# Attention and FFN kernel: low parts of W ahead of tile 0's gate, tile 0's LoRA inside tile 1, and tile 1's y transposed by DMA

## The chip, the cores and the metric

The kernel runs on one core of one Trainium2 chip. The metric is the device time of one execution in microseconds, and smaller is better. One core has a matrix engine (PE), a vector engine (DVE), a scalar engine (ACT), GpSimd (POOL) and SyncE (SP), which here issues nearly all transfers.

## The reference

With x of (2, 512, 1024) and ctx of (2, 1024, 1024), the reference quantises, multiplies, and then adds a linear layer with a mixture of eight rank-16 LoRA experts, of which each row uses two:

```python
q1 = fake_quant(layernorm(x)); q2 = fake_quant(ctx)      # uint8 grids, scale and zero point are inputs
x1 = x + q1 @ q2
y = layernorm(x1)
logits = y @ W_router.T; top 2 of 8 experts, their softmax weights renormalised -> combine (row, expert)
h = einsum('nd,erd->ner', y, A_stack) * combine[..., None]
out = x1 + y @ W_base.T + b_base + 2.0 * einsum('ner,eor->no', h, B_stack)
```

## The kernel before

The 1,024 rows are cut into eight tiles of 128 rows (T = 8), and the 1,024 columns of the contraction into eight slices k (K = 8). Every engine has its own instruction stream, written out by hand. An engine executes its stream in order, and semaphores hold an instruction until what it names has happened. So the order of the calls in each engine's block is the schedule.

**Stage 1** makes x1. For each tile PE multiplies the transposed quantised x (`a1_t`) with the quantised ctx (`product`), DVE takes the sum out of PSUM into `xs` (`sum_x1`), and either DVE or POOL adds a correction that depends on the column (`add_corr`).

**Stage 2** multiplies y with W. To get more than 16 bits of precision, y and W are each split into a rounded half (`_hi`) and the rest (`_lo`), both float16, and `wide(t, k)` issues six matmuls of 512 columns: hi·hi, hi·lo and lo·hi, for each half of the output. `narrow(t)` does the same against A and the router (`ar_hi`, `ar_lo`, 136 columns, 24 matmuls). From its result DVE works out the gate (`gate_tile`, 14 small instructions) and the weighted LoRA rows `hc`. PE transposes `hc` (`transpose_hc`), ACT and DVE split it (`split_hct`), and `lora(t)` multiplies it with B (six matmuls of 512 columns), into the same PSUM banks as `wide`.

**W's halves.** Eight slices of W lie in `stage`. When the largest value is known (`peaks_w` on DVE, one PE matmul, `scale_w` on DVE), ACT rounds each slice (`split_w` on ACT writes `w_hi`) and DVE makes the rest (`split_w` on DVE writes `w_lo`). For tile 0, PE takes slice k when `w_lo` of k is there.

**The way of y.** DVE measures a tile's mean and variance (`statistics_y`), POOL turns them into a scale and a bias (`scale_y`), and ACT makes y (`make_y`). For tiles 0 and 1, PE transposes y in float32 and ACT and DVE split the transposed tile (`split_first_yt`, `split_yt`). From tile 2 on, ACT rounds y (`round_y` writes `y_hi`), DVE makes the rest (`rest_y` writes `y_lo`; both lie in the buffer `a1_t`, so the trace names them a_t), and SP sends each half through a transposing DMA into `yt_hi` and `yt_lo`, which raises `y_hi_turned` and `y_lo_turned`.

Each output tile is closed by DVE: `add_bias` adds bias and a row term to `xs`, `sum_out` adds the PSUM banks, and SP stores it.

Of the kernel before, what the change touches and what calls it, by code (L numbers as in the profile page):

```python
# [5 lines left out]
P = 128  # L6
# [23 lines left out]
def xattn_ffn(nc, x, ctx_kv, quant, w_t, bias, ar_t, b_t, out):  # L30
# [20 lines left out]
    with ExitStack() as stack:  # L51
# [86 lines left out]
        HCT = slice(256, 256 + P)  # L138
# [3 lines left out]
        FIRST_ADDS = 3  # L142
# [48 lines left out]
        @block.sync  # L191
        def _(sp):
            def load_x(t):
                sp.dma_start(xs[:, t, :], x_tiles[t]).then_inc(x_in[t], 16)

            def load_staged(n):
                if n >= RING:
                    sp.wait_ge(ctx_ready, n - RING + 1)
                src = ctx_tiles[n] if n < N else w_tiles[n - N]
                sp.dma_start(stage[:, n % RING, :], src).then_inc(stage_in[n % RING], 16)  # L200

            def transpose_y(t):
                sp.wait_ge(out_done, t - 1)
                sp.wait_ge(y_hi_ready, t - 1)
                sp.dma_start_transpose(out=yt_hi[:, t % 2, :, :], in_=y_hi).then_inc(y_hi_turned, 16)
                sp.wait_ge(y_lo_ready, t - 1)
# [36 lines left out]
        def _(pool):
# [68 lines left out]
            scale_y(0, 2)  # L312
            pool.wait_ge(b_lo_ready, 1)
            add_corr(3)
            scale_y(2, 3)
            add_corr(4)
            scale_y(3, 4)
            for t in range(5, T):
                add_corr(t)
                scale_y(t - 1, t)  # L320
# [3 lines left out]
        def _(act):  # L324
# [52 lines left out]
            def make_y(t):  # L377
                act.wait_ge(y_scaled, t + 1)
                if t > 0:
                    act.wait_ge(y_transposed, min(t, 2))  # L380
                if t > 2:
                    act.wait_ge(y_lo_ready, t - 2)
                nc.scalar.activation(y[:, :], xs[:, t, :], ACT.Identity, bias=y_bias[:, t:t + 1],  # L383
                                     scale=y_scale[:, t:t + 1]).then_inc(y_ready, 1)
# [7 lines left out]
            def split_yt(t):  # L392
                act.wait_ge(y_transposed, t + 1)
                nc.scalar.activation(yt_hi[:, t % 2, :, :].rearrange("p (h k) c -> p h (k c)", h=2),
                                     ps[:, YT_BANKS, :], ACT.Copy).then_inc(yt_hi_ready, 1)

            def round_y(t):
                if t > 2:
                    act.wait_ge(y_hi_turned, 16 * (t - 2))
# [8 lines left out]
            def split_hct(t):  # L408
                act.wait_ge(hc_transposed, t + 1)
                nc.scalar.activation(hct_hi[:, :], ps[:, AR_BANK, HCT], ACT.Copy).then_inc(hct_hi_ready, 1)  # L410
# [24 lines left out]
            make_y(1)  # L435
            split_b()
            for k in range(3, K):
                split_w(k)
            gate_weight(0)
            split_yt(1)  # L440
# [3 lines left out]
            for t in range(1, T):  # L444
                gate_weight(t)
                if t + 1 < T:
                    make_y(t + 1)
                    round_y(t + 1)
                split_hct(t)
# [4 lines left out]
        def _(dve):  # L454
# [168 lines left out]
            def split_yt(t):  # L623
                def halves(a):
                    return a.rearrange("p (h k) c -> p h (k c)", h=2)

                dve.wait_ge(yt_hi_ready, t + 1)
                nc.vector.tensor_tensor(halves(yt_lo[:, t % 2, :, :]), ps[:, YT_BANKS, :],
                                        halves(yt_hi[:, t % 2, :, :]), ALU.subtract).then_inc(yt_lo_ready, 1)

            def rest_y(t):
                dve.wait_ge(stage1_done, T)
                dve.wait_ge(y_ready, t + 1)
                dve.wait_ge(y_hi_ready, t - 1)
                if t > 2:
                    dve.wait_ge(y_lo_turned, 16 * (t - 2))
# [136 lines left out]
        def _(pe):  # L773
# [160 lines left out]
            pe.wait_ge(y_hi_turned, 16 * (last - 1))  # L934
            pe.wait_ge(y_lo_turned, 16 * (last - 1))
# [37 lines left out]
```

## Time and profile before

| what | value |
|---|---|
| median of 3 runs | 171.85 us (171.85 to 171.87) |
| the profiled execution | 171.81 us |
| its span, from first to last instruction | 170.0 us |
| around the span | 1.81 us |
| busy: PE, DVE, ACT, POOL | 158.2, 118.9, 74.1, 59.9 us |

The profiled execution stands 0.04 us below the median. Times in rows are microseconds from the span's start. In a timeline, a row is a run of instructions of one line: start, duration from the first start to the last end, engine, line, operation, output and input, count, and in brackets the idle time of the engine before it and what ended it. Matmuls overlap: a matmul of 512 columns shows 0.38 us, but the next one starts earlier than its end.

### The profile page before, as it was taken

Reading aid. Unit: us, or ns where it says so; the run is one execution under the profiler, and the core shown is the slowest. Engines: PE = TensorE matmul, PEld = TensorE weight load, DVE = VectorE, ACT = ScalarE, POOL = GpSimd, SP = SyncE. Lnnn points to the kernel's source line nnn. Section 1 sums busy time; section 2 is a strip of 40 time slices with the busy share of each in tenths; the row PEclk is TensorE's granted clock in tenths of the full one; section 3 lists DMA queues with packets and bytes.
Section 4 is the critical chain, followed back from the end, with each engine's and each line's share of the span. In section 5 each row is a group of like instructions: output and inputs, shape, how many; then the busy total and the mean of one; then the engine's idle time right before and its main releaser. Section 6 shows DMA issues by size and latency. Waiting matters only on the chain.

```text
span 170.0 us, 2585 instructions
## 1 busy us (share of the span) xinstructions
PE 158.2 (93%) x922; PEld 83.6 (49%) x922; DVE 118.9 (70%) x276; ACT 74.1 (44%) x100; POOL 59.9 (35%) x140
## 2 busy tenths in 40 slices
PE   6977898899989799799999999999999999999992
PEld 3543344345535356364554564564555556456541
DVE  7993939999998999996919908908907826804802
ACT  3096509799996994506217007105305305300000
POOL 8905476887840000187082081082050050000000
PEclk9999999999999999999999999999999999999998
DMA  4999999999930000000352250350360360360311
GB/s 111 387 416 413 406 409 407 406 411 413 407 151 2 0 0 4 0 0 0 75 177 41 46 160 10 72 169 0 62 185 4 62 185 0 62 185 6 123 62 62
DMA packets 19452, 25.89 MB, mean 152 GB/s; under 512 B 13552, under 2 KB 13808, under 8 KB 19440
## 3 DMA queue, kind: packets, MB, share of 16 engines
q1 hardware_dynamic: 19296, 25.73, 43.4%
q8 instruction: 7, 0.11, 0.3%
q14 instruction: 5, 0.04, 0.1%
q10 hardware_dynamic: 144, 0.00, 0.0%
HBM read 18.38 MB, written 4.19 MB: 133 GB/s over the span
## 4 chain that ended last, share of the span: by engine, by line
PE 62%; DVE 19%; issue 6%; POOL 5%; ACT 4%; DMA 2%; DVEq 0%; ACTq 0%; POOLq 0%
PE ps L835 37%; PE ps L795 10%; PE ps L825 5%; DVE w_lo L606 2%; PE ps L786 2%; DVE xs L541 2%; ACT w_hi L370 2%; DMA yt_lo<-a_t 2%; PE ps L816 2%; PE ps L817 2%; PE ps L818 2%; POOL root L262 2%; PE ps L780 1%; DVE bnx L472 1%; DVE bnx L470 1%
## 5 line engine op out<-in xcount | busy, mean ns | idle before, releaser
L835 PE MATMUL ps<-w_hi,yt_hi 128*128 128x512 f16 x128 | 39.5, 380 | 1.7 <-DVE w_lo L606 1.2
L835 PE MATMUL ps<-w_lo,yt_hi 128*128 128x512 f16 x128 | 39.4, 379 | 0.0
L835 PE MATMUL ps<-w_hi,yt_lo 128*128 128x512 f16 x128 | 39.4, 379 | 0.0
L795 PE MATMUL ps<-a,a_t 128*128 128x512 f16 x128 | 31.2, 379 | 2.3 <-DVE a_t L534 1.5
L406 ACT ACTIVATE gate<-gate,ar_undo 128x1 f32<-128x1 f32 x8 | 2.4, 295 | 55.9 <-DVE gate L643 55.9
L331 ACT ACTIVATE a<-stage,prm,inv_s 128x1024 uint8<-128x1024 f32 x16 | 19.4, 1241 | 9.4 <-DMA stage<-in_ctx_kv 9.3
L642 DVE MAX8 top<-ps 128x8 f32<-128x8 f32 x8 | 1.4, 173 | 27.5 <-PE ps L818 27.5
L835 PEld LDWEIGHTS ps<-w_hi,yt_lo 128*128 128x128 f16 x128 | 12.5, 98 | 15.1
L795 PEld LDWEIGHTS ps<-a,a_t 128*128 128x128 f16 x128 | 11.9, 98 | 16.2 <-DVE a_t L534 3.0
L835 PEld LDWEIGHTS ps<-w_lo,yt_hi 128*128 128x128 f16 x128 | 12.5, 98 | 14.7
L250 POOL TENSOR_TENSOR xs<-xs,corr 128x1024 f32<-128x1024 f32 x5 | 11.8, 2363 | 22.2 <-DVE b_lo L612 22.2
L835 PEld LDWEIGHTS ps<-w_hi,yt_hi 128*128 128x128 f16 x128 | 11.6, 98 | 14.9 <-issue 2.8
L261 POOL TENSOR_SCALAR root<-mvy 128x1 f32<-128x1 f32 (+1 forms) x7 | 1.5, 218 | 38.8 <-DVE mvy L466 38.7
L816 PE MATMUL ps<-ar_hi,yt_hi 128*128 128x136 f16 x64 | 11.7, 223 | 0.2 <-DMA yt_lo<-a_t 0.2
L817 PE MATMUL ps<-ar_lo,yt_hi 128*128 128x136 f16 x64 | 11.7, 223 | 0.0
L818 PE MATMUL ps<-ar_hi,yt_lo 128*128 128x136 f16 x64 | 11.7, 223 | 0.0
L383 ACT ACTIVATE y<-xs,y_bias,y_scale 128x1024 f32<-128x1024 f32 x8 | 9.8, 1228 | 1.8 <-POOL y_bias L289 1.8
L671 DVE SCALAR_TENSOR_TENSOR xs<-xs,row_term,bias_sb 128x1024 f32<-128x1024 f32 x8 | 10.3, 1285 | 0.3
L786 PE MATMUL ps<-a,ones 128*128 128x512 f16 x32 | 9.5, 379 | 0.9 <-ACT a L331 0.9
L606 DVE SCALAR_TENSOR_TENSOR w_lo<-stage,scale,w_hi 128x1024 f16<-128x1024 f32 x8 | 10.0, 1279 | 0.2 <-ACT w_hi L370 0.2
L541 DVE SCALAR_TENSOR_TENSOR xs<-ps,con,xs 128x1024 f32<-128x1024 f32 x8 | 10.1, 1268 | 0.0
L262 POOL TENSOR_TENSOR root<-root,minus_half 128x1 f32<-128x1 f32 (+1 forms) x13 | 9.7, 744 | 1.1
(135 smaller groups left out, 262.4 us busy)
## 6 DMA issues: line engine op xcount, KB each, us to landing
stage<-in_ctx_kv SPq DMA_DIRECT2D x16, 512.0 KB, 13.2
stage<-in_w_t SPq DMA_DIRECT2D x8, 512.0 KB, 10.7
xs<-in_x SPq DMA_DIRECT2D x7, 512.0 KB, 13.2
out_dram<-xs SPq DMA_DIRECT2D x7, 512.0 KB, 3.0
ar_raw<-in_ar_t SPq DMA_DIRECT2D x1, 544.0 KB, 16.3
xs<-in_x SPq DMA_DIRECT2D x2, 256.0 KB, 3.8
b_raw<-in_b_t SPq DMA_DIRECT2D x1, 512.0 KB, 11.3
bias_sb<-in_bias SPq DMA_DIRECT2D x1, 512.0 KB, 12.1
```

Source lines behind the costliest of these rows:

```text
L250: nc.gpsimd.tensor_tensor(xs[:, t, :], xs[:, t, :], corr[:, t // TB, :], ALU.add).then_inc(x1_ready, 1)
L262: then(nc.gpsimd.tensor_tensor(guess, whole, minus_half[:, w], ALU.pow))
L331: nc.scalar.activation(low_bytes(a2[:, n, :]), stage[:, n % RING, :], ACT.Identity, bias=prm[:, 3:4], scale=inv_s[:, 2:3]).then_inc(ctx_re ...
L541: nc.vector.scalar_tensor_tensor(out=xs[:, t, :].rearrange("p (h n) -> p h n", h=NH), in0=ps[:, s1_bank(t):s1_bank(t) + 2, :], scalar=s12, ...
L606: nc.vector.scalar_tensor_tensor(out=w_lo[:, k, :], in0=stage[:, k, :], scalar=scale[:, 2:3], in1=w_hi[:, k, :], op0=ALU.mult, op1=ALU.sub ...
L671: nc.vector.scalar_tensor_tensor(out=xs[:, t, :], in0=xs[:, t, :], scalar=row_term[:, t:t + 1], in1=bias_sb[:, :], op0=ALU.add, op1=ALU.ad ...
L786: last = nc.tensor.matmul(ps[:, COLSUM_BANK + h, :], ones16[:, 0:P], a2[:, b * K + k, h * H:(h + 1) * H], start=k == 0, stop=k == K - 1)
L795: last = nc.tensor.matmul(ps[:, s1_bank(t) + h, :], a1_t[:, t % 4, k, :], a2[:, n, h * H:(h + 1) * H], start=k == 0, stop=k == K - 1)
L816: nc.tensor.matmul(dst, yt_hi[:, p, k, :], ar_hi[:, k, :], start=k == 0, stop=False)
L817: nc.tensor.matmul(dst, yt_hi[:, p, k, :], ar_lo[:, k, :], start=False, stop=False)
L818: last = nc.tensor.matmul(dst, yt_lo[:, p, k, :], ar_hi[:, k, :], start=False, stop=k == K - 1)
L835: ins = nc.tensor.matmul(ps[:, OUT_BANK[p] + h, :], part, rhs[:, k, h * H:(h + 1) * H], start=k == 0 and part is hi and rhs is w_hi, stop= ...
```

## The change

Seven things change together:

- Tile 1's y no longer goes through PE. It takes the way of the later tiles: `round_y(1)` on ACT, `rest_y(1)` on DVE, two transposing DMAs on SP. `split_yt` is gone from ACT and DVE.
- `add_corr(2)` moves from DVE to POOL, and on POOL `scale_y(t - 1)` now stands ahead of `add_corr(t)` for t = 3 and 4 as well.
- On DVE, `take_a1t(7)` moves ahead of `peaks_w`; `split_ar` moves from ahead of the first `split_w` to behind the fourth; and all eight `split_w` now stand ahead of `gate_tile(0)`, with `rest_y(1)` among them.
- On ACT, `split_b` moves behind the last `split_w`, and for t = 1 alone `split_hct(1)` moves ahead of `make_y(2)`.
- On PE, `narrow(0)` moves from behind slice 3 to behind slice 5, `transpose_hc(0)` and `lora(0)` move into tile 1, and `narrow(1)` moves from ahead of tile 1 to behind its slice 2. `transpose_hc(1)` moves from behind slice 2 to behind slice 6, and `lora(1)` to the end of tile 1.
- For t = 1, DVE does `split_hct(1)` ahead of `sum_out(0)`.
- The transposed `hc` gets a bank of its own, and six filling matmuls ahead of stage 2 become two.

```diff
-        HCT = slice(256, 256 + P)
+        HCT_BANK = 3
+        HCT = slice(0, P)
...
-        FIRST_ADDS = 3
+        FIRST_ADDS = 2
...
             def transpose_y(t):
-                sp.wait_ge(out_done, t - 1)
-                sp.wait_ge(y_hi_ready, t - 1)
+                if t >= 2:
+                    sp.wait_ge(out_done, t - 1)
+                sp.wait_ge(y_hi_ready, t)
...
             sp.dma_start(bias_sb[:, :], bias.partition_broadcast(P)).then_inc(bias_in, 16)
+            transpose_y(1)
...
             scale_y(0, 2)
+            pool.wait_ge(w_diag_ready, 1)
+            add_corr(2)
             pool.wait_ge(b_lo_ready, 1)
-            add_corr(3)
-            scale_y(2, 3)
-            add_corr(4)
-            scale_y(3, 4)
-            for t in range(5, T):
+            for t in range(3, T):
+                scale_y(t - 1, t)
                 add_corr(t)
-                scale_y(t - 1, t)
...
             make_y(1)
+            for k in range(3, 6):
+                split_w(k)
+            round_y(1)
+            for k in range(6, K):
+                split_w(k)
             split_b()
-            for k in range(3, K):
-                split_w(k)
             gate_weight(0)
-            split_yt(1)
             split_hct(0)
             sum_row(0)
             sum_row(1)
             for t in range(1, T):
                 gate_weight(t)
+                if t == 1:
+                    split_hct(t)
                 if t + 1 < T:
                     make_y(t + 1)
                     round_y(t + 1)
-                split_hct(t)
+                if t > 1:
+                    split_hct(t)
...
             scale_ar()
-            add_corr(2)
             sum_x1(5)
+            take_a1t(7)
             peaks_w()
-            take_a1t(7)
             scale_w()
-            split_ar()
             sum_x1(6)
             split_w(0)
             split_first_yt()
             split_w(1)
             split_w(2)
             split_w(3)
+            split_ar()
+            split_w(4)
             sum_x1(7)
...
-            split_w(4)
             split_w(5)
+            rest_y(1)
+            split_w(6)
+            split_w(7)
             dve.wait_ge(expert_ready, 1)
             gate_tile(0)
-            split_w(6)
-            split_w(7)
             split_hct(0)
             split_b()
-            split_yt(1)
             statistics_y(2)
             add_bias(0)
             for t in range(1, T):
                 gate_tile(t)
-                sum_out(t - 1)
-                split_hct(t)
+                if t == 1:
+                    split_hct(t)
+                    sum_out(t - 1)
+                else:
+                    sum_out(t - 1)
+                    split_hct(t)
...
-            keep_busy(6, 5)
+            keep_busy(2, 5)
...
                 wide(0, k, False)
-                if k == 3:
+                if k == 5:
                     pe.wait_ge(x1_summed, T)
-                    pe.wait_ge(yt_lo_ready, 1)
                     pe.wait_ge(ar_lo_ready, 2)
                     narrow(0)
+
+            pe.wait_ge(y_hi_turned, 16)
+            pe.wait_ge(y_lo_turned, 16)
+            for k in range(K):
+                wide(1, k, False)
+                if k == 1:
+                    transpose_hc(0)
+                if k == 2:
+                    narrow(1)
                 if k == 3:
-                    transpose_y(1)
-                if k == 5:
-                    transpose_hc(0)
-            pe.wait_ge(b_lo_ready, 1)
-            lora(0, stop=True)
-
-            for t in range(1, T - 1):
-                if t == 1:
-                    pe.wait_ge(yt_lo_ready, 2)
...
+                    pe.wait_ge(b_lo_ready, 1)
+                    lora(0, stop=True)
+                if k == 6:
+                    transpose_hc(1)
+            lora(1, stop=True)
```

ACT's stream of before, from tile 0's gate weight on. Here `gate` is the gate weight, `hct_hi` is `split_hct`, `junk,rowsum` is `sum_row`, `y` is `make_y` and `a_t` is `round_y`; the last three rows are `make_y(2)`, `round_y(2)` and `split_hct(1)`.

```order
L406 ACTIVATE gate<-gate,ar_undo 128x1 [waits gate_diff]
L394 ACTIVATE yt_hi<-ps 128x1024 [waits y_transposed]
L410 ACTIVATE hct_hi<-ps 128x128 [waits hc_transposed]
L345 ACTIVATE junk,rowsum<-a 128x1024 [waits peaks_act,x_quantised] x2
L406 ACTIVATE gate<-gate,ar_undo 128x1 [waits gate_diff]
L383 ACTIVATE y<-xs,y_bias,y_scale 128x1024 [waits y_transposed,y_scaled]
L402 ACTIVATE a_t<-y 128x1024 [waits y_ready,stage1_done]
L410 ACTIVATE hct_hi<-ps 128x128 [waits hc_transposed]
```

The same place after the change.

```order
L402 ACTIVATE gate<-gate,ar_undo 128x1 [waits gate_diff]
L406 ACTIVATE hct_hi<-ps 128x128 [waits hc_transposed]
L346 ACTIVATE junk,rowsum<-a 128x1024 [waits peaks_act,x_quantised] x2
L402 ACTIVATE gate<-gate,ar_undo 128x1 [waits gate_diff]
L406 ACTIVATE hct_hi<-ps 128x128 [waits hc_transposed]
L384 ACTIVATE y<-xs,y_bias,y_scale 128x1024 [waits y_lo_ready,y_transposed,y_scaled]
L398 ACTIVATE a_t<-y 128x1024 [waits y_ready,stage1_done,y_hi_turned]
```

`split_hct(1)`, which waits for PE to transpose tile 1's `hc`, has moved ahead of `make_y(2)` and `round_y(2)`; the transposed tile's split is gone.

PE's stream of before, from `transpose_hc(0)` to the first matmuls of `narrow(1)`.

```order
L810 MATMUL ps<-ident,hc 128x128
L835 MATMUL ps<-w_hi,yt_hi 128x512 x2
L835 MATMUL ps<-w_lo,yt_hi 128x512 x2
L835 MATMUL ps<-w_hi,yt_lo 128x512 x2
L835 MATMUL ps<-w_hi,yt_hi 128x512 x2
L835 MATMUL ps<-w_lo,yt_hi 128x512 x2
L835 MATMUL ps<-w_hi,yt_lo 128x512 x2
L825 MATMUL ps<-b_hi,hct_hi 128x512 x2
L825 MATMUL ps<-b_lo,hct_hi 128x512 x2
L825 MATMUL ps<-b_hi,hct_lo 128x512 x2
L816 MATMUL ps<-ar_hi,yt_hi 128x136
```

PE's stream after the change, from `transpose_hc(1)` to the first matmul of `narrow(2)`.

```order
L806 MATMUL ps<-ident,hc 128x128
L831 MATMUL ps<-w_hi,yt_hi 128x512 x2
L831 MATMUL ps<-w_lo,yt_hi 128x512 x2
L831 MATMUL ps<-w_hi,yt_lo 128x512 x2
L821 MATMUL ps<-b_hi,hct_hi 128x512 x2
L821 MATMUL ps<-b_lo,hct_hi 128x512 x2
L821 MATMUL ps<-b_hi,hct_lo 128x512 x2
L812 MATMUL ps<-ar_hi,yt_hi 128x136
```

Before, five slices of `wide(1)` and `lora(1)` stood between `transpose_hc(1)` and tile 2; now it is one slice and `lora(1)`.

## Rows read from the trace of the kernel before

**Rows 1.** The page, busy time of each engine (share of the span, instructions)

```profile
PE 158.2 (93%) x922; PEld 83.6 (49%) x922; DVE 118.9 (70%) x276; ACT 74.1 (44%) x100; POOL 59.9 (35%) x140
```

**Rows 2.** Chain that ended last, 78 to 102: start, time, engine and line

```profile
78.02 1.25 ACT y L383
...
80.81 0.28 DVE row_term L667
...
82.31 1.23 DVE a_t L637
83.56 3.03 DMA yt_lo<-a_t
...
86.72 0.22 PE ps L816
...
92.37 3.88 PE ps L835 x18
96.26 1.39 PE ps L825 x6
97.65 2.60 PE ps L835 x12
...
101.67 0.43 PE ps L835 x2
```

**Rows 3.** Timeline around the end of stage 1, three engines

```profile
47.70 1.23 DVE L550 TENSOR_TENSOR xs<-xs,corr 128x1024 f32<-128x1024 f32 x1
...
48.44 0.61 PE L780 MATMUL ps<-ident,a 128*128 128x128 f16 x8
...
51.20 0.23 PE L878 MATMUL ps<-diag,ones_b 128*128 128x128 bf16 x1 [0.85 <-DVE a_t L534]
...
52.79 1.15 ACT L370 ACTIVATE w_hi<-stage,scale 128x1024 f16<-128x1024 f32 x1 [1.25 <-DVE scale L601]
```

**Rows 4.** Timeline of ACT, 57 to 65

```profile
57.11 1.23 ACT L383 ACTIVATE y<-xs,y_bias,y_scale 128x1024 f32<-128x1024 f32 x1
...
59.19 5.30 ACT L370 ACTIVATE w_hi<-stage,scale 128x1024 f16<-128x1024 f32 x5
```

**Rows 5.** Timeline of DVE, 57 to 76

```profile
57.71 2.48 DVE L606 SCALAR_TENSOR_TENSOR w_lo<-stage,scale,w_hi 128x1024 f16<-128x1024 f32 x2
...
65.22 0.17 DVE L642 MAX8 top<-ps 128x8 f32<-128x8 f32 x1
...
67.70 2.47 DVE L606 SCALAR_TENSOR_TENSOR w_lo<-stage,scale,w_hi 128x1024 f16<-128x1024 f32 x2
...
70.29 1.22 DVE L612 TENSOR_TENSOR b_lo<-b_raw,b_hi 128x1024 fp32r<-128x1024 f32 x1
...
75.45 0.17 DVE L642 MAX8 top<-ps 128x8 f32<-128x8 f32 x1
```

**Rows 6.** Timeline, tile 0's `hc` from PE to ACT

```profile
67.90 0.27 PE L810 MATMUL ps<-ident,hc 128*128 128x128 f32 x1
68.21 0.28 ACT L410 ACTIVATE hct_hi<-ps 128x128 fp32r<-128x128 f32 x1 [1.33 <-PE ps L810]
```

**Rows 7.** Timeline of POOL and DVE, `add_corr(5)` beside tile 2's gate

```profile
87.86 2.36 POOL L250 TENSOR_TENSOR xs<-xs,corr 128x1024 f32<-128x1024 f32 x1
...
88.55 0.21 DVE L643 TENSOR_SCALAR gate<-top 128x1 f32<-128x1 f32 x1
...
88.95 1.30 DVE L646 CAST top_f<-top_i 128x8 f32<-128x8 uint32 x1
```

**Rows 8.** Busy time by stretch at the end; the number behind POOL's is the granted clock

```profile
166.50:167.00 0.50, 0.21 (x1) 0.00 (x0) 0.26 (x1) 0.00 (x0) 0.00 (x0) 1.00 0.00 0
...
168.50:169.00 0.50, 0.00 (x0) 0.00 (x0) 0.00 (x0) 0.00 (x0) 0.00 (x0) 0.68 0.80 270
```

**Rows 9.** Line 842, the matmuls of the start, 1 to 4 and 4 to 8: ns min/median/max

```profile
L842 PE MATMUL ps<-ones x9: 503/527/527, 1.4 to 4.0; 128*128 128x384 f16 x9
...
L842 PE MATMUL ps<-ones x24: 326/326/527, 3.7 to 8.0; 128*128 128x384 f16 x24
```

More of the change, by code:

```diff
@@ L202, in transpose_y @@
             def transpose_y(t):
-                sp.wait_ge(out_done, t - 1)
-                sp.wait_ge(y_hi_ready, t - 1)
+                if t >= 2:
+                    sp.wait_ge(out_done, t - 1)
+                sp.wait_ge(y_hi_ready, t)
                 sp.dma_start_transpose(out=yt_hi[:, t % 2, :, :], in_=y_hi).then_inc(y_hi_turned, 16)
-                sp.wait_ge(y_lo_ready, t - 1)
+                sp.wait_ge(y_lo_ready, t)
                 sp.dma_start_transpose(out=yt_lo[:, t % 2, :, :], in_=y_lo).then_inc(y_lo_turned, 16)
@@ L379, in make_y @@
                 if t > 0:
-                    act.wait_ge(y_transposed, min(t, 2))
-                if t > 2:
-                    act.wait_ge(y_lo_ready, t - 2)
+                    act.wait_ge(y_transposed, 1)
+                if t > 1:
+                    act.wait_ge(y_lo_ready, t - 1)
                 nc.scalar.activation(y[:, :], xs[:, t, :], ACT.Identity, bias=y_bias[:, t:t + 1],
@@ L390, in split_first_yt @@
                                          ps[:, YT_BANKS.start + h, :], ACT.Copy).then_inc(ready, 1)
[L392 to L395, printed above, removed]
             def round_y(t):
-                if t > 2:
-                    act.wait_ge(y_hi_turned, 16 * (t - 2))
+                if t > 1:
+                    act.wait_ge(y_hi_turned, 16 * (t - 1))
                 act.wait_ge(stage1_done, T)
@@ L409, in split_hct @@
                 act.wait_ge(hc_transposed, t + 1)
-                nc.scalar.activation(hct_hi[:, :], ps[:, AR_BANK, HCT], ACT.Copy).then_inc(hct_hi_ready, 1)
+                nc.scalar.activation(hct_hi[:, :], ps[:, HCT_BANK, HCT], ACT.Copy).then_inc(hct_hi_ready, 1)
             act.dma_start(prm[:, :], quant.partition_broadcast(P)).then_inc(quant_in, 16)
@@ L448, in _ @@
                     round_y(t + 1)
-                split_hct(t)
+                if t > 1:
+                    split_hct(t)
                 if t + 1 < T:
@@ L621, in split_first_yt @@
                                             ALU.subtract).then_inc(lo_ready, 1)
[L623 to L629, printed above, removed]
             def rest_y(t):
@@ L633, in rest_y @@
                 dve.wait_ge(y_ready, t + 1)
-                dve.wait_ge(y_hi_ready, t - 1)
-                if t > 2:
-                    dve.wait_ge(y_lo_turned, 16 * (t - 2))
+                dve.wait_ge(y_hi_ready, t)
+                if t > 1:
+                    dve.wait_ge(y_lo_turned, 16 * (t - 1))
                 nc.vector.tensor_tensor(y_lo, y[:, :], y_hi, ALU.subtract).then_inc(y_lo_ready, 1)
@@ L661, in split_hct @@
                 dve.wait_ge(hct_hi_ready, t + 1)
-                nc.vector.tensor_tensor(hct_lo[:, :], ps[:, AR_BANK, HCT], hct_hi[:, :].bitcast(F32),
+                nc.vector.tensor_tensor(hct_lo[:, :], ps[:, HCT_BANK, HCT], hct_hi[:, :].bitcast(F32),
                                         ALU.subtract).then_inc(hct_lo_ready, 1)
@@ L809, in transpose_hc @@
                 pe.wait_ge(hc_ready, t + 1)
-                nc.tensor.transpose(ps[:, AR_BANK, HCT], hc[:, :], ident[:, :]).then_inc(hc_transposed, 1)
+                nc.tensor.transpose(ps[:, HCT_BANK, HCT], hc[:, :], ident[:, :]).then_inc(hc_transposed, 1)
             def narrow(t):
@@ L904, in _ @@
                 wide(0, k, False)
-                if k == 3:
+                if k == 5:
                     pe.wait_ge(x1_summed, T)
-                    pe.wait_ge(yt_lo_ready, 1)
                     pe.wait_ge(ar_lo_ready, 2)
                     narrow(0)
-                if k == 3:
-                    transpose_y(1)
-                if k == 5:
-                    transpose_hc(0)
-            pe.wait_ge(b_lo_ready, 1)
-            lora(0, stop=True)
-            for t in range(1, T - 1):
-                if t == 1:
-                    pe.wait_ge(yt_lo_ready, 2)
-                else:
-                    pe.wait_ge(y_hi_turned, 16 * (t - 1))
-                    pe.wait_ge(y_lo_turned, 16 * (t - 1))
+            pe.wait_ge(y_hi_turned, 16)
[6 more added lines that the diff above has]
+                    narrow(1)
+                if k == 3:
+                    pe.wait_ge(b_lo_ready, 1)
[3 more added lines that the diff above has]
+            lora(1, stop=True)
+            for t in range(2, T - 1):
+                pe.wait_ge(y_hi_turned, 16 * t)
+                pe.wait_ge(y_lo_turned, 16 * t)
                 narrow(t)
-                if t >= 2:
-                    pe.wait_ge(out_summed, t - 1)
+                pe.wait_ge(out_summed, t - 1)
                 for k in range(K):
@@ L933, in _ @@
             last = T - 1
-            pe.wait_ge(y_hi_turned, 16 * (last - 1))
-            pe.wait_ge(y_lo_turned, 16 * (last - 1))
+            pe.wait_ge(y_hi_turned, 16 * last)
+            pe.wait_ge(y_lo_turned, 16 * last)
             narrow(last)
```

## The prediction

> **What bounds the kernel now.** I read the busy time of the engines first: PE works 158.2 of 170.0 us [rows 1], so time can only come from the 12 us in which it stands. Then the chain that ended last, to see where PE does not lead [rows 2]. From 86.72 on every link is PE's: `narrow(2)` starts there, 18 matmuls of `wide` take 3.88 (one slice of six 1.29), `lora` takes 1.39, the last two slices end at 100.25, and the first `wide` of the next tile starts at 101.67, which makes a `narrow` 1.42. A tile is 8 x 1.29 + 1.42 + 1.39 and a transpose, 13.3 us, and nothing in the diff changes PE's work from tile 2 on. Ahead of 86.72 the link is another: y of tile 2 is made on ACT at 78.02, its rest on DVE at 82.31, the transposing DMA takes 3.03, and then PE starts. So the question is where the start of `narrow(2)` moves.
>
> **The end of stage 1.** PE stands 0.85 ahead of the matmul of line 878 at 51.20, for the a1_t that DVE takes late [rows 3]. DVE does `add_corr(2)` from 47.70 for 1.23 first. With that gone and `take_a1t(7)` ahead of `peaks_w`, it can take the tile when PE's transposes end, 48.44 + 0.61 = 49.05. PE's own earlier products last until about 50.3, so 0.9 is gained and no more. From line 878 to ACT's first `w_hi` lie 1.59 (51.20 to 52.79), so that starts at 51.9. POOL's `add_corr(2)`, 2.36 like the one of [rows 7], runs from 50.3 to 52.7; POOL stands idle there in any case.
>
> **DVE's queue.** `sum_x1(6)` starts at 51.8 and the first `w_lo` at 53.05, when `w_hi` is there (51.9 + 1.15). An instruction of 1,024 columns starts 1.20 behind the last (two in 2.48 [rows 5]), and so do the two halves of tile 0's y. That brings DVE to its fourth `w_lo` at 57.85. ACT has by then made `w_hi` 0, tile 0's halves, `w_hi` 1 and 2, and y(1) (1.23 [rows 4], 1.1 until the next start), and makes slice 3 from 57.3 to 58.45 (1.15, five in 5.30 [rows 4]): DVE waits 0.6. Then come slice 3, `split_ar` (two instructions over 1,088 columns, 1.4 at the same rate and with a second start), slice 4, `sum_x1(7)` and slice 5, whose result is there at 64.85; `rest_y(1)` ends at 66.0; slices 6 and 7 end at 68.3, and only there does `gate_tile(0)` start. Before it was 65.22 [rows 5]. That is -0.9, +1.1 for `rest_y(1)`, +2.4 for two `w_lo`, +0.5 for the longer wait.
>
> **PE in tiles 0 and 1.** It is fed by `w_lo` and stands in pieces of up to 1.3 us until slice 5 starts at 64.9. Slice 5, `narrow(0)` and two slices are 3 x 1.29 + 1.42: PE is at 70.2. y(1)'s rest has landed at 66.0 + 3.03 + 0.14 = 69.2, so the new wait is hidden by 1.0; if that cover were gone, each microsecond would count. Removing the eight transposes of y(1) and four filling matmuls costs and gives nothing by itself, as PE waits for `w_lo` anyway. In tile 1 follow two slices (72.8), `transpose_hc(0)`, a slice, `narrow(1)` (75.6), a slice (76.9), `lora(0)` (78.3) and three slices: `transpose_hc(1)` starts at 82.2. Two more waits could delay it. DVE does `split_hct(0)` at 73.4, 0.6 behind the transpose (0.31 to ACT, 0.28 there [rows 6]), and `b_lo` (1.22) is ready at 74.9, wanted at 76.9. From `b_lo`'s start to the next gate were 5.16 (70.29 to 75.45 [rows 5]), now less by `split_yt`; so `gate_tile(1)` starts by 78.8 and, with 2.5 for a gate (65.22 to 67.70), `hc` is there by 81.4. Both fit.
>
> **The new wait.** The order rows of ACT show `split_hct(1)` ahead of `make_y(2)`. An engine executes in order, so y(2), whose scale is ready near 80.2 (from `b_lo`'s start at 73.6 the same way as 70.29 to 78.02, less 1.1 for `split_yt`), is not begun before PE has transposed `hc(1)` at 82.2; before, `make_y(2)` went at 78.02 with four slices of PE's work behind it still to come. Queued behind the waiting `split_hct` are `make_y(2)` and `round_y(2)`; on DVE, behind its own `split_hct(1)`, are `sum_out(0)`, `add_bias(1)` and `rest_y(2)`. From PE's transpose on: 0.31 to ACT, 0.28 `hct_hi`, 0.21 `hct_lo` on DVE, 1.20 `sum_out(0)`, 1.50 from the row term to the rest of y (80.81 to 82.31), 1.23 `rest_y(2)`, and 3.18 from its end (83.54) to PE's start (86.72) [rows 2, 6]. Sum 7.9. ACT's branch (0.31, then y and its rounding, about 2.4) is ready sooner than DVE's 3.5. Meanwhile PE has one transpose, one slice and `lora(1)`, 2.8 us. It then **stands 5.1 us**, and this gap doesn't depend on how early PE comes there. `narrow(2)` starts at 82.2 + 7.9 = 90.1 in place of 86.72: **+3.4**.
>
> After that each tile needs what it needed. In the loop from tile 2 on the order on ACT and DVE is as before; POOL's `scale_y(3)` follows `statistics_y(3)` at the same distance from `narrow(2)`, and the `add_corr` behind it merely moves by a tile. I price these at nothing; the cover is PE's 13.3 us per tile.
>
> **The clock.** At the end of the trace the last matmul ends at 166.71 and the granted clock is full until about 168.68 (a mean of 0.68 over half a microsecond, between 1.00 and 0.50): it fell from 2.4 to 1.2 GHz, 2.0 us after PE's last work [rows 8]. A stand of 5.1 is longer than that. At the start the first matmuls of line 842 last 527 ns up to 4 us and 326 later [rows 9]: about 3.1 us of work, from 1.45 on, went at the lower level, 1.2 GHz. If `narrow(2)` begins in that way, half of 3.1 is lost, **+1.5**. The bounds are 0, if the clock stays up, and 2.5, if the low stretch is as long as the stand itself. I take 1.5, as it is a measured stretch of work behind idleness.
>
> **Sum:** 171.81 (the profiled execution, 0.04 below the median) + 3.4 + 1.5 = 176.7 us.
>
> **The rivals.**
>
> *The clock stays up* through the stand: 171.81 + 3.4 = 175.2. For it: where the clock falls may vary, and two microseconds at the end is one sample. Against it: 5.1 is two and a half times that.
>
> *POOL's `add_corr(2)` holds `scale_w`.* It now runs beside DVE's small instructions that make W's scale. In [rows 7] a cast of 8 elements takes 1.30 and ends with POOL's `add_corr` at 90.2. If the one-element instructions of `scale_w` are held in this way from 50.9 to 52.7, everything behind W's scale is 1.8 later, 171.81 + 3.4 + 1.5 + 1.8 = 178.5. Against it: line 643, with one element, took 0.21 in the middle of the same `add_corr`. The Trainium skill has the rule (SBUF — State Buffer, "Who interferes with whom"): a tensor_scalar in a two-port mode and a GpSimd instruction lock each other out, "the other fully blocks"; by the rule alone the scale would wait and the sum would be this rival's. The trace agrees for the cast and not for one element, so it gets a small chance.
>
> *The clock falls in tile 0 too.* Between 61.1 and 64.9 PE has by my times one slice in 3.8 us, thinner than anything in the trace of before. With a second low stretch: 178.3.
>
> *y(2) is not late,* and the kernel is faster. If `make_y(2)` could start by 77.5, PE would go from the end of tile 1 at 85.0 straight into `narrow(2)`, 1.7 ahead of before: 170.1. For it: in all else PE is ahead. Against it: the order rows; break-even would need `transpose_hc(1)` at 78.8, and even a PE that is never held in tile 0 from 55.0 on, where tile 0's first half is ready, only comes to 78.8.
>
> **How the numbers follow.** The main case has 0.66, the clock that stays up 0.16, POOL's hold 0.06, a second fall of the clock 0.06, the faster case 0.04, and 0.02 is left for no change. A measurement of this kernel tells 0.2% (0.35 us) from nothing. Slower is then 0.94, same 0.02, faster 0.04. The range 174.9 to 178.3 holds the first two cases with 0.3 us for errors in the early times, up to 2.5 for the clock, and the fourth case's middle.
>
> **What the changed kernel's profile would show.** Line 878's counterpart at 50.3; `gate_tile(0)` at 68.3; the DMA of y(1) landed a microsecond before `wide(1)` starts at 70.2; `transpose_hc(1)` at 82.2 with ACT's `make_y(2)` right behind it; PE idle for 5.1 us ahead of `narrow(2)`, released by the DMA of y_lo; a granted clock below 1.00 around 88 to 93; and from the next tile on a period of 13.3. The prediction is wrong if `make_y(2)` starts well before `transpose_hc(1)`, if PE reaches that transpose before 79, or if the clock's loss is not between 0 and 2.5.

## The result, and the profile after

| what | before | after |
|---|---|---|
| median | 171.85 us (171.84 to 171.87) | 177.70 us (176.94 to 177.96) |
| ratio, 95% interval | | 1.0333 (1.0299 to 1.0368) |
| the profiled execution, its span | 171.81, 170.0 us | 176.94, 175.2 us |

The changed kernel is 5.85 us slower; 176.7 was predicted, with a range of 174.9 to 178.3. The profiled execution is the shortest of the four, which matters for the clock below.

The page first, to be held against [rows 1]: the busy time by engine, and TensorE's granted clock in 40 slices of the span.

```profile
PE 157.9 (90%) x910; PEld 83.6 (48%) x910; DVE 116.7 (67%) x275; ACT 74.1 (42%) x100; POOL 61.4 (35%) x141
...
PEclk9999999999999999999978999999999999999999
```

PE does as much work as before in a longer span, so the time is standing time. The two low digits of the clock, slices 21 and 22 of 4.4 us, say where to look. The chain that ended last, 60 to 105, answers to [rows 2].

```profile
64.92 1.15 DVE a_t L630
66.08 4.56 DMA yt_lo<-a_t
...
70.78 2.75 PE ps L831 x12
...
82.94 0.12 PE ps L806
83.09 0.29 ACT hct_hi L406
...
83.61 1.27 DVE xs L670
84.88 0.19 DVE row_term L660
85.09 0.63 DVE xs L664
...
86.30 1.23 DVE a_t L630
87.54 3.04 DMA yt_lo<-a_t
...
90.72 0.27 PE ps L812
```

Read it from the bottom. `narrow(2)` starts at 90.72 and not at 86.72; ahead of it is the DMA of y_lo, ahead of that `rest_y(2)`, `add_bias(1)` (row term and L664), `sum_out(0)` (L670), and ahead of those PE's transpose of `hc(1)` (its matmul starts at 82.78 in the timeline; the chain counts its last part). In [rows 2] no link of PE's stands between 78.02 and the DMA. Now it also has an earlier one: the DMA of tile 1's y_lo, 4.56 us long, ahead of `wide(1)`.

The timeline at the places that the prediction named, with the engine's idle time and what ended it in brackets; these answer to [rows 3, 5, 7].

```profile
50.38 0.22 PE L874 MATMUL ps<-diag,ones_b 128*128 128x128 bf16 x1
...
50.32 2.36 POOL L253 TENSOR_TENSOR xs<-xs,corr 128x1024 f32<-128x1024 f32 x1 [1.81 <-DVE diag L555]
...
51.97 1.15 ACT L371 ACTIVATE w_hi<-stage,scale 128x1024 f16<-128x1024 f32 x1 [0.52 <-DVE scale L602]
...
58.59 1.28 DVE L607 SCALAR_TENSOR_TENSOR w_lo<-stage,scale,w_hi 128x1024 f16<-128x1024 f32 x1 [0.57 <-ACT w_hi L371]
...
68.37 0.16 DVE L635 MAX8 top<-ps 128x8 f32<-128x8 f32 x1
...
83.26 1.23 ACT L384 ACTIVATE y<-xs,y_bias,y_scale 128x1024 f32<-128x1024 f32 x1
...
90.72 0.27 PE L812 MATMUL ps<-ar_hi,yt_hi 128*128 128x136 f16 x1 [4.99 <-DMA yt_lo<-a_t]
...
93.38 0.59 PE L831 MATMUL ps<-w_hi,yt_hi 128*128 128x512 f16 x2
```

The last two rows are the stand and what follows it: `narrow(2)` takes 2.66 us to the first `wide` matmul, where it took 1.42 before. The windows around it show why; the number behind POOL's is the granted clock.

```profile
88.00:90.00 2.00, 0.00 (x0) 0.00 (x0) 0.92 (x3) 0.00 (x0) 0.80 (x3) 0.99 0.82 168
90.00:91.00 1.00, 0.28 (x3) 0.32 (x4) 0.00 (x0) 0.00 (x0) 0.75 (x4) 0.50 1.02 403
91.00:93.00 2.00, 2.00 (x20) 2.00 (x19) 0.00 (x0) 0.00 (x0) 1.74 (x5) 0.50 0.11 45
93.00:94.00 1.00, 1.00 (x9) 0.68 (x7) 0.38 (x4) 0.00 (x0) 1.00 (x1) 0.82 0.06 16
```

While PE stood, the clock fell from 2.4 to 1.2 GHz (at about 89.95: 0.99 is a mean over two microseconds, 1.00 and then 0.50), and it was back at about 93.36. So the 5.13 us that the profiled execution is longer than the one before are a late start of 4.0 and some 1.1 to 1.2 of slow matmuls. The median is 0.7 longer still.

### The profile page after: what moved, and what is told of

Its sections match the earlier page's. It is cut to its first block, busy times and chain, and to the rows that moved or that the text cites. A ratio compares the mean times of both kernels' runs of the same rounds, so it can differ in the third digit from the quotient of the medians.

```text
span 175.2 us, 2567 instructions
## 1 busy us (share of the span) xinstructions
PE 157.9 (90%) x910; PEld 83.6 (48%) x910; DVE 116.7 (67%) x275; ACT 74.1 (42%) x100; POOL 61.4 (35%) x141
## 4 chain that ended last, share of the span: by engine, by line
PE 67%; DVE 16%; DMA 4%; POOL 3%; issue 3%; ACT 3%; DVEq 0%; ACTq 0%; POOLq 0%
PE ps L831 41%; PE ps L791 10%; PE ps L821 6%; DMA yt_lo<-a_t 4%; PE ps L812 2%; PE ps L782 2%; PE ps L813 2%; DVE xs L542 2%; PE ps L814 2%; ACT w_hi L371 2%; DVE w_lo L607 2%; PE ps L776 1%; DVE bnx L473 1%; DVE bnx L471 1%; DVE a_t L630 1%
## 5 line engine op out<-in xcount | busy, mean ns | idle before, releaser
L812 PE MATMUL ps<-ar_hi,yt_hi 128*128 128x136 f16 x64 | 12.8, 234 | 5.0 <-DMA yt_lo<-a_t 5.0
L253 POOL TENSOR_TENSOR xs<-xs,corr 128x1024 f32<-128x1024 f32 x6 | 14.1, 2353 | 1.8 <-DVE diag L555 1.8
L813 PE MATMUL ps<-ar_lo,yt_hi 128*128 128x136 f16 x64 | 12.8, 235 | 0.0
L814 PE MATMUL ps<-ar_hi,yt_lo 128*128 128x136 f16 x64 | 12.8, 234 | 0.0
L664 DVE SCALAR_TENSOR_TENSOR xs<-xs,row_term,bias_sb 128x1024 f32<-128x1024 f32 x8 | 10.3, 1284 | 0.3
```

Source lines behind the costliest of these rows:

```text
L253: nc.gpsimd.tensor_tensor(xs[:, t, :], xs[:, t, :], corr[:, t // TB, :], ALU.add).then_inc(x1_ready, 1)
L664: nc.vector.scalar_tensor_tensor(out=xs[:, t, :], in0=xs[:, t, :], scalar=row_term[:, t:t + 1], in1=bias_sb[:, :], op0=ALU.add, op1=ALU.ad ...
L812: nc.tensor.matmul(dst, yt_hi[:, p, k, :], ar_hi[:, k, :], start=k == 0, stop=False)
L813: nc.tensor.matmul(dst, yt_hi[:, p, k, :], ar_lo[:, k, :], start=False, stop=False)
L814: last = nc.tensor.matmul(dst, yt_lo[:, p, k, :], ar_hi[:, k, :], start=False, stop=k == K - 1)
```

## The experiments

A yardstick for all of them: PE's start of `narrow(2)`, 86.72 before. If nothing behind it changes, the time is 171.81 plus the shift of that start. "Left" is what the profiled execution took beyond that.

| kernel | `narrow(2)` at | by the shift | profiled | left | median (range) |
|---|---|---|---|---|---|
| the changed kernel | 90.72 | 175.81 | 176.94 | 1.13 | 177.70 (176.94 to 177.96) |
| e1, ACT's order of before | 90.29 | 175.38 | 178.11 | 2.73 | 177.75 (177.29 to 178.36) |
| e2, `rest_y(2)` early on DVE | 90.49 | 175.58 | 176.45 | 0.87 | 176.42 (176.32 to 176.90) |
| e3, both edits | 87.56 | 172.65 | 173.55 | 0.90 | 173.57 (173.45 to 173.75) |
| e4, e3 and statistics earlier | 86.20 | 171.29 | 172.47 | 1.18 | 172.47 (172.42 to 172.69) |
| e5, filled stand | 91.13 | 176.22 | 176.12 | -0.10 | 176.12 (175.25 to 176.40) |
| e6, only the end of stage 1 | 86.16 | 171.25 | 171.25 | 0.00 | 171.25 (171.24 to 171.27) |
| e7, scale rows behind the gates | 85.84 | 170.93 | 170.88 | -0.05 | 170.78 (170.56 to 171.06) |
| e8, `transpose_hc(1)` earlier | 89.13 | 174.22 | 175.80 | 1.58 | 175.83 (175.68 to 175.86) |
| e9, e7 with the fetch moved | 85.32 | 170.41 | 170.31 | -0.10 | 170.32 (170.31 to 170.34) |

**Which stream holds y(2)?** e1 restores ACT's order of before and leaves DVE's. e2 leaves ACT's and puts `sum_out(0)` and `rest_y(2)` ahead of DVE's waiting `split_hct(1)`; e3 has both edits. On DVE this is a new order and not that of before, in which `rest_y(2)` stood behind `split_hct(1)` and `add_bias(1)` too.

```diff
 # e1 and e3, ACT
                 gate_weight(t)
-                if t == 1:
-                    split_hct(t)
                 if t + 1 < T:
                     make_y(t + 1)
                     round_y(t + 1)
-                if t > 1:
-                    split_hct(t)
+                split_hct(t)
 # e2 and e3, DVE
-                if t == 1:
-                    split_hct(t)
-                    sum_out(t - 1)
-                else:
-                    sum_out(t - 1)
-                    split_hct(t)
+                sum_out(t - 1)
+                if t == 1:
+                    rest_y(t + 1)
+                split_hct(t)
                 add_bias(t)
-                if t + 1 < T:
+                if 1 < t and t + 1 < T:
                     rest_y(t + 1)
```

> The changed kernel with ACT's order of before for tile 1: make_y(2) and round_y(2) ahead of split_hct(1); DVE's stream is untouched. My theory: the stand of PE ahead of narrow(2) is held by two streams. ACT's part is undone here, but on DVE rest_y(2) still stands behind split_hct(1), sum_out(0) and add_bias(1), so narrow(2) starts 7.9 us behind transpose_hc(1) as in the changed kernel (about 90.7), and the time stays at 177.7 (176.9 to 178.0). Rival: ACT's order alone is the cause, as the prediction's heading of the new wait has it; then y_lo of tile 2 starts at about 83.3, narrow(2) at about 87.7, and the time is near 172.8.

Measured: 177.75 us, ratio 1.0341 (1.0310 to 1.0372). The chain of e1:

```profile
80.36 1.25 ACT y L384
81.71 0.98 ACT a_t L398
82.69 0.25 ACT hct_hi L406
...
83.17 1.28 DVE xs L667
...
84.80 1.07 issue
85.87 1.23 DVE a_t L627
87.11 3.04 DMA yt_lo<-a_t
```

y(2) is made at 80.36, 2.9 earlier than in the changed kernel, and it buys nothing: DVE's `split_hct(1)` still waits for PE, and `sum_out(0)`, the row term, `add_bias(1)` and `rest_y(2)` follow it. `narrow(2)` starts 7.95 behind the transpose, as in the changed kernel (7.94). ACT's new order is not what holds it; DVE's queue is. Of that queue only `sum_out(0)` (L667, 1.28) got behind the wait by the change. With the true order of before on both engines, which no run has, I estimate from this chain a start 7.95 - 1.28 = 6.7 behind the transpose. So by this estimate most of the stand comes from PE's later `transpose_hc(1)`, and the new orders add to it.

> The changed kernel with sum_out(0) and rest_y(2) ahead of split_hct(1) and add_bias(1) on DVE; ACT's stream is untouched. My theory: make_y(2) still starts 0.5 us behind transpose_hc(1), its rounding ends 2.9 behind it, rest_y(2) follows at once, and narrow(2) starts 2.9 + 1.2 + 3.2 = 7.3 behind transpose_hc(1), 0.6 less than in the changed kernel: near 90.1 and a time near 177.1. Rival: DVE's order alone is the cause; then narrow(2) starts near 87.5 and the time is near 172.8.

Measured: 176.42 us, ratio 1.0274 (1.0257 to 1.0291), 0.7 below the expected 177.1. With DVE free, ACT holds; the timeline of e2:

```profile
83.42 1.23 ACT L384 ACTIVATE y<-xs,y_bias,y_scale 128x1024 f32<-128x1024 f32 x1
...
86.02 1.23 DVE L630 TENSOR_TENSOR a_t<-y,a_t 128x1024 f16<-128x1024 f32 x1 [3.86 <-ACT a_t L398]
```

`make_y(2)` starts right behind `hct_hi`, and `narrow(2)` at 90.49. The distance from the transpose (82.94) shrinks only from 7.94 to 7.55, and the start moves by 0.2. The median is 1.3 below the changed kernel's, but most of that I put down to the clock: three of e2's four executions have a mean granted clock of 0.987 to 0.990, and three of the changed kernel's four have 0.981. Of the 0.87 left, 0.37 is a wait of PE for `hc(2)`, of the kind that e3 shows next.

> Both edits: on ACT make_y(2) and round_y(2), on DVE sum_out(0) and rest_y(2), stand ahead of split_hct(1). My theory: make_y(2) then starts when POOL's scale is there, at 80.8, y_hi is there at 83.2, rest_y(2) ends at 84.4 and narrow(2) starts at 87.6. PE stands about 2.2 us in place of 5.3, the clock stays up or loses under 0.5 us, and the time is 172.7 (172.4 to 173.3). Rival: the stand comes from something else (the DMA, POOL); then no more than 0.6 us comes back.

Measured: 173.57 us, ratio 1.0103 (1.0086 to 1.0120). Only with both edits does the start move far, by 3.2, to 87.56. The clock stays at 1.00 and 4.1 of the 5.85 us are gone. That is 0.9 more than the expected 172.7 and outside its range, and the trace of e3 has the place:

```profile
90.39 2.36 POOL L253 TENSOR_TENSOR xs<-xs,corr 128x1024 f32<-128x1024 f32 x1
...
90.85 1.93 DVE L640 TENSOR_SCALAR c<-expert,top_f,gate 128x8 f32<-128x8 f32 x1
92.69 0.20 DVE L641 TENSOR_SCALAR gate<-gate 128x1 f32<-128x1 f32 x1
...
93.80 0.33 PE L801 MATMUL ps<-ident,hc 128*128 128x128 f32 x1 [0.77 <-DVE hc L645]
```

An instruction of 8 elements in tile 2's gate, 0.29 elsewhere, lasts until POOL's `add_corr` is over, and PE waits 0.77 for `hc(2)`. The change did reorder POOL (`scale_y(t - 1)` now stands ahead of `add_corr(t)` for every t from 3 on, not for 3 and 4 alone), but an `add_corr` right behind `scale_y(3)` was there before as well: it began 1.14 behind the start of `narrow(2)` and held a cast of tile 2's gate for 1.30 [rows 7], and PE did not wait. In the changed kernel it is 1.14 again. In e3 it is 2.83 (90.39 against 87.56), since e3 puts `split_hct(1)` and `add_bias(1)` between `rest_y(2)` and `statistics_y(3)`, on which `scale_y(3)` waits. So the new moment comes with e3's own order; how much POOL's reordering has in it is not shown.

**Does an earlier y(2) pay?** e4 is e3 with `statistics_y(2)` and `split_b` ahead of `split_hct(0)`.

> As the third experiment, and on DVE split_b and statistics_y(2) stand ahead of split_hct(0), where the changed kernel lets DVE idle for 3.1 us. My theory: the statistics are there near 73.5, POOL's scale near 77.4, make_y(2) starts there, y_lo is turned before tile 1 ends at 85.5, and narrow(2) starts without a stand of more than 0.2: 85.5 to 85.7 in place of 86.7 in the kernel before, time 170.7 (170.4 to 171.0), faster than before. Rival: a wait that was in the shadow of the stand comes out (gate of tile 1, the sum of tile 0), and the time stays at 171.5 or more.

Measured: 172.47 us, ratio 1.0043 (1.0029 to 1.0057); 170.7 was missed. `narrow(2)` starts at 86.20 (85.5 to 85.7 was expected), 0.5 ahead of the kernel before. But L640 takes 2.09 in tile 1's gate and 2.20 in tile 2's, both begun inside an `add_corr`, and PE waits 1.04 for `hc(2)`. That wait turns the lead over the kernel before into a loss of 0.6.

**Does `add_corr` do that?** e7 is e3 with `statistics_y(2)` ahead of `split_b` and `split_hct(0)`, and with each `add_corr` held until the gate is through:

```diff
-            pool.wait_ge(b_lo_ready, 1)
             for t in range(3, T):
-                scale_y(t - 1, t)
+                pool.wait_ge(hc_ready, t - 2)
                 add_corr(t)
+                scale_y(t - 1, t)
```

> As the fourth experiment, with statistics_y(2) ahead of split_b, and with POOL's add_corr(t) held until hc of tile t - 2 is made and put ahead of scale_y(t - 1). The fourth experiment lost 1.0 us at transpose_hc(2) and 2.1 us in gate 1, each inside add_corr. My theory: with add_corr right behind a gate no small instruction of a gate falls into it, transpose_hc(2) is not waited for, narrow(2) starts at 85.0 to 85.6, and the time is 170.6 (170.2 to 171.0). Rival: the loss at the gates has another cause; then it stays and the time is 172 or more.

Measured: 170.78 us, ratio 0.9939 (0.9922 to 0.9955), and on a second chip 170.83, 0.9945 (0.9928 to 0.9961). This beats the kernel before, though `narrow(2)` starts at 85.84 and not by 85.6. The timeline of e7 at tile 2's gate:

```profile
89.12 0.29 DVE L640 TENSOR_SCALAR c<-expert,top_f,gate 128x8 f32<-128x8 f32 x1
...
90.47 2.37 POOL L253 TENSOR_TENSOR xs<-xs,corr 128x1024 f32<-128x1024 f32 x1 [0.87 <-DVE hc L645]
```

L640 is back at 0.29, PE doesn't wait for `hc(2)`, and nothing is left beyond the shift. The overlap has not gone, it has moved: `b_lo` now takes 2.16 and `rest_y(2)` 1.85 where they took 1.22 or so, each beside an `add_corr`, and there PE has no wait from it.

**What the clock costs.** e5 puts 32 filling matmuls between `lora(1)` and `narrow(2)` of the changed kernel.

```diff
+            keep_busy(32, 6)
             for t in range(2, T - 1):
                 pe.wait_ge(y_hi_turned, 16 * t)
```

> The changed kernel with 32 filling matmuls (384 columns, into a bank that nobody reads any more) between lora(1) and narrow(2): PE works through the stand but nothing arrives sooner. My theory: the stand costs its length (narrow(2) at 90.1 to 90.8 in place of 86.72, +3.4 to +4.0) and the fall of the clock costs the rest of the +5.85. With the fillers the granted clock stays at 1.00, narrow(2) starts where it did, and the time is 175.6 (175.2 to 176.0), with little scatter. Rival: the clock is not what makes the rest (the later tiles are slower for another reason, such as GpSimd's new places); then the time stays at 177 or more.

Measured: 176.12 us, ratio 1.0239 (1.0208 to 1.0270), 0.1 above the expected range. The granted clock stays at 1.00 and the late start alone explains the time, since nothing is left. `narrow(2)` starts at 91.13 and not at 90.72. It is 8.65 behind the transpose (82.48) and not 7.95, because tile 2's two transposing DMAs take 4.7 and 3.7 us here, with a packet of DMA queue q8 between 87.9 and 88.2 (e9 is about that). By the same sum without the clock the changed kernel would take 171.81 + 4.0 = 175.8, so its median holds 1.9 us of clock. This is a remainder: it takes for granted that the other executions start `narrow(2)` at 90.72 too. The plain difference of the two medians is 1.6.

**Is the distance fixed?** e8 is the changed kernel with `transpose_hc(1)` behind slice 5 and not slice 6.

> The changed kernel with transpose_hc(1) one slice earlier, behind slice 5 in place of slice 6. My theory: narrow(2) follows transpose_hc(1) by 7.9 us wherever that stands, so it starts 1.3 us sooner (89.4 beside 90.7), the stand shrinks from 5.3 to about 4.0, and the time falls by 1.3 to 176.4; if the shorter stand also saves the clock, to 174.6. Rival: narrow(2) waits for something that doesn't hang on transpose_hc(1), and the time stays at 177.7.

Measured: 175.83 us, ratio 1.0232 (1.0215 to 1.0249), 0.6 below the expected 176.4. The timeline of e8:

```profile
81.18 0.27 PE L806 MATMUL ps<-ident,hc 128*128 128x128 f32 x1
...
89.13 0.22 PE L812 MATMUL ps<-ar_hi,yt_hi 128*128 128x136 f16 x1 [3.71 <-DMA yt_lo<-a_t]
```

From the transpose to `narrow(2)` it is 7.95 again, so the 1.6 us by which the transpose comes sooner are won in full. The stand shrinks to 3.71 us, and the clock is still at 1.2 GHz from about 89.9 to 93.3. Of the 0.6, 0.3 is `wide(1)`, which starts at 70.48 in place of 70.78.

**What is the end of stage 1 worth alone?** e6 is the kernel before with three edits only: `add_corr(2)` on POOL, `take_a1t(7)` ahead of `peaks_w`, and FIRST_ADDS = 2.

> The kernel before with one part of the change alone: add_corr(2) on POOL as soon as the peak of W is known, and take_a1t(7) ahead of peaks_w on DVE. My theory: the last tile of stage 1 starts on PE 0.8 us sooner (50.4 for 51.20), W's scale with it, everything to the start of narrow(2) moves by that, and the time is 171.0 (170.9 to 171.3). Rival: POOL's add_corr(2) holds the small instructions of scale_w or something behind them; then the time is 171.8 or more.

Measured: 171.25 us, ratio 0.9967 (0.9954 to 0.9979). Of the 0.87 won there (`w_hi` at 51.92 for 52.79), 0.56 reaches `narrow(2)` and the end. The timeline of e6 shows a loss on the way:

```profile
51.86 2.05 DVE L588 SCALAR_TENSOR_TENSOR ar_lo<-ar_raw,scale,ar_hi 128x1024 f16<-128x1024 f32 x2
...
50.27 2.36 POOL L250 TENSOR_TENSOR xs<-xs,corr 128x1024 f32<-128x1024 f32 x1 [1.84 <-DVE diag L556]
```

`split_ar` (1.48 at the same place in the kernel before) takes 2.05 with its start inside POOL's `add_corr`, which ends at 52.63, and `sum_x1(6)` behind it starts only 0.30 earlier than before. The small instructions of W's scale ahead of it, with one element each, keep their 0.14 to 0.20.

**Why 4.56 us for one DMA?** In the eight traces before this one that have it, tile 1's y_lo is issued at about 66.0 and takes 4.2 to 4.8, where the median of the seven y_lo of the changed kernel is 3.0. In each, a packet of DMA queue q8, whose kind the view calls instruction, falls inside its flight: in 67.0 to 68.0, and in e2 in 68.0 to 69.0. The text below calls e7's order on VectorE that of the kernel before; it is that of e3, with `statistics_y(2)` ahead. e9 is e7 with 36 matmuls of 32 columns in PE's idle pieces of tile 0, to move that packet; the same kernel without them ran beside it.

```diff
+                if k in (3, 4, 5):
+                    for _ in range(12):
+                        nc.tensor.matmul(ps[:, 5, 0:32], ones16[:, 0:P], ones16[:, 0:32], start=True, stop=True)
                 pe.wait_ge(w_lo_ready, k + 1)
```

> The kernel of the run before it in this study (scale rows on GpSimd behind the gates, ScalarE and VectorE in the order of the kernel before, 170.78 us) with 36 matmuls of 32 columns into an unused corner of PSUM, 12 each ahead of three waits for W's low parts in tile 0, where TensorE stands idle anyway. They compute nothing that is used; each moves the later packets of queue q8 earlier. Theory: the packet of q8 that falls at about 67 us is what makes the DMA of tile 1's y_lo, issued at about 66.0, take 4.2 to 4.8 us. With no packet inside its flight it lands in 3.0 to 3.2 us, at about 69.2, TensorE's wait of 0.33 us ahead of tile 1's first wide matmul goes, and the time is 170.4 us; if the packet falls into the flight of y_hi (61.6 to 64.7) instead, that one takes over 4 us. Rival: the length belongs to that place (what the cores' other engines do then), wherever the packet is: the DMA issued at 66.0 takes 4.2 to 4.8 again and the time is 170.8 us.

> The same kernel without the 36 small matmuls, on the same chip, to compare with. 170.8 us; the DMA of tile 1's y_lo issued at about 66.0 takes 4.2 to 4.8 us and a packet of q8 lies inside its flight.

Measured: 170.32 us against 170.83. The DMA queues by stretch, with packets, MB and the share of time of the 16 engines. First the kernel without the small matmuls: 66.0 to 67.2 has no packet, and these are 67.2 to 68.6 and, behind the dots, 68.6 to 70.6.

```profile
q1 hardware_dynamic: 938, 0.24, 208.3%
q8 instruction: 1, 0.02, 6.0%
...
q1 hardware_dynamic: 118, 0.02, 7.8%
```

Then e9: 66.0 to 67.2, 67.2 to 68.6, and 68.6 to 70.6.

```profile
q8 instruction: 1, 0.02, 5.0%
...
q1 hardware_dynamic: 1053, 0.26, 96.7%
...
q1 hardware_dynamic: 3, 0.00, 0.1%
```

The two transfers have the same number of packets, 1,056. With the packet of q8 ahead of them, all but three are through by 68.6 and it lands in 3.0. With that packet among them, their time doubles and 118 of them, more than a tenth, come after 68.6. So the packet may fall just behind the DMA's issue, as in e9 (66.05 to 66.10), and cost nothing: it costs when it falls among the transfer's packets. Other transfers in these traces lie between: with the q8 packet 0.5 us behind the issue (e9's y_hi at 143.22) it was 3.4, with 0.8 (e5's y_lo at 87.25) 3.7. One of 3.5 has none of q8 (y_hi at 80.49 in the kernel before), so q8 is not the only thing that can lengthen one. The rival, that the length belongs to the place, is out: e9's DMA is issued at 66.1, beside the same work of PE and DVE.

## Why the prediction came true, and where it was off

**The end of stage 1, DVE's queue.** As predicted: line 878's counterpart 50.38 (50.3), first `w_hi` 51.97 (51.9), DVE's wait 0.57 (0.6), `gate_tile(0)` 68.37 (68.3).

**PE in tiles 0 and 1.** Slice 5 was right (64.98; 64.9). "y(1)'s rest has landed at 66.0 + 3.03 + 0.14 = 69.2, so the new wait is hidden by 1.0" is the step that failed. The 3.03 is mis-sized: 4.56 was measured, the cover of 1.0 was used up, and `wide(1)` started at 70.78 and not at 70.2. e9 against its companion puts the price of that packet at 0.5 us. The trace of before had such a case, tile 4's y_hi, issued at 104.84. Its DMA view, 106.0 to 107.5 and then 107.5 to 109.5 (the packets), and the landing:

```profile
q1 hardware_dynamic: 1035, 0.26, 90.1%
q8 instruction: 1, 0.02, 4.0%
...
q1 hardware_dynamic: 21, 0.00, 2.5%
...
yt_hi<-a_t SPq DMA_TRANSPOSE x1, 4.6
```

Here 21 packets come late, without the doubled share, and it is 4.6 all the same. I took one duration for a transfer that has two. From there `transpose_hc(1)` came at 82.78 (82.2).

**The new wait.** The 7.9 from transpose to `narrow(2)` was 7.9 (7.94 in the changed kernel, 7.95 in e1 and e8), and the stand was 4.99 against 5.1. The mechanism is shown: the distance stays at 7.9 wherever the transpose stands (e8), and e3 takes most of the wait away by orders alone. The one longer distance, e5's 8.65, has slower DMAs in it. The prediction named both streams and said that DVE's branch is the longer; e1 and e2 bear that out, and that either alone holds nearly as long. Its paragraph opens with ACT's order, which would have misled anyone who undid just that: it is worth nothing by itself. Nor does it say that DVE's `rest_y(2)` stood behind `split_hct(1)` before as well, so that by the estimate at e1 PE's later transpose is the larger part. Behind `narrow(2)` the tiles did keep their period: tile 3's, 4's and 5's y_hi are issued at 96.71, 109.99 and 123.28, 13.3 apart.

**The clock.** The mechanism was right, the size too small for the median: 1.5 predicted, 1.2 in the profiled execution, 1.9 in the median. The changed kernel's own longest execution has 2.15, inside the bound of 2.5. But e1, whose stand is as long (5.00), has 2.73 left in its profiled execution, so 2.5 was no bound. Its windows:

```profile
88.00:90.00 2.00, 0.00 (x0) 0.00 (x0) 0.49 (x2) 0.00 (x0) 1.14 (x4) 0.81 0.94 227
90.00:93.00 3.00, 2.71 (x25) 2.74 (x26) 0.00 (x0) 0.00 (x0) 2.57 (x7) 0.50 0.30 116
93.00:96.00 3.00, 3.00 (x10) 1.04 (x9) 2.11 (x12) 2.22 (x3) 0.76 (x1) 0.50 0.01 3
96.00:98.00 2.00, 2.00 (x11) 0.92 (x10) 1.32 (x2) 0.26 (x1) 0.00 (x0) 0.98 0.24 49
```

It is low for some 6.8 us there, twice the 3.4 of the changed kernel's profile. The changed kernel's other three executions have a mean granted clock of 0.981 over the span and its profiled one 0.990; half speed for 6.7 us in 175.7 gives the first, for 3.4 the second. I read these as the long form and the short one. The form does not set the time alone: in e1, 177.39 has 0.981 and 177.29 has 0.990. What picks between them was not tried.

**The rivals.** The clock that stays up: refuted by the windows. POOL's `add_corr(2)` holding `scale_w`: refuted, those instructions kept their 0.14 to 0.20, in the changed kernel and in e6. But POOL's later `add_corr` did hold others, where the prediction priced POOL's order at nothing. For the changed kernel itself nothing was right: PE has no wait for `hc(2)` there. In e2, e3 and e4 it waits 0.37, 0.77 and 1.04. The Trainium skill has both halves (SBUF — State Buffer, "Who interferes with whom"): an instruction of DVE's with two inputs in SBUF contends with a GpSimd instruction that reads SBUF; and of a tensor_scalar in a two-port mode and a GpSimd instruction, the one that issues first shuts the other out for the whole of its length. The traces agree with 2.05 for `split_ar` in place of 1.48, and with 1.93 to 2.20 for L640 with 8 elements. Its counterpart with one element was not held: line 641 of e2, at 93.69 inside an `add_corr` from 93.29 to 95.64, kept 0.21. A second fall of the clock in tile 0: refuted, 1.00 throughout. The faster case: y(2) was late, as argued.

**The sum.** 4.0 us of late start (3.4 predicted; 0.5 of the difference is the long DMA) and 1.9 of clock (1.5) make the 5.9 that were measured. The 1.9 is the remainder, so only the first term is checked by this sum; e5's windows at 1.00 check the second.

## What to carry to other kernels

When an instruction waits for something that the change makes later, list what stands behind it on every engine, and free all of them together: here each of two streams held the next tile by itself. Freeing one moved `narrow(2)` by 0.4 (e1) and 0.2 us (e2), freeing both by 3.2. The 0.4 comes from an earlier `transpose_hc(1)` alone. Price the last link by its whole distribution, not by its median, when its cover is near one microsecond. And look for what a faster path will run beside: e9 is 1.5 us faster than the kernel before. e6 has 0.6 of that alone, and the rest came only when y(2) was early and POOL's long instruction was kept away from the gate.

## What the runs showed of the hardware

- A transposing DMA of 1,056 packets mostly lands in 3.0 to 3.2 us. With a packet of the instruction queue q8 1.2 to 2.6 us behind its issue it took 4.1 to 4.8; moving that packet by 1.7 us (67.8 to 66.1) took 4.5 down to 3.0. The spread of the kernel's time went with it, from 170.67 to 171.00 down to 170.31 to 170.34. That q8 brings PE's instructions is inferred: added matmuls moved it.
- After a stand, TensorE's clock was low for 3.4 us or for some 6.8. The low stretch cost 0.5 (e2), 1.1 (the changed kernel), 1.6 (e8) and 2.7 us (e1) in the profiled executions. In e3, with waits of 0.54 and 1.31, it stayed at 1.00.
- In e8 the clock fell at about 89.9, when PE had already been back at work for 0.8 us (`narrow(2)` at 89.13) after a stand of 3.71.
- Beside GpSimd's `add_corr` (128x1024), VectorE's tensor_scalar of 128x8 took up to 2.20 us in place of 0.29, and one of 128x1 kept 0.21.
